# The output projection of the preceding batch, moved in among the transposes of an attention stage

## The reference

```python
x = x + L0_ffn(L0_cond(x, cond_256))     # attention, then a product-key expert layer
x = x + L1_ffn(L1_cond(x, cond_256))     # two small mixtures of 8 experts
```

```python
qkv = (x @ Wqkv.T + bqkv)                       # 16 heads of 8 channels
attn = softmax(q @ k.T / sqrt(8))               # 128 x 128 for each head and batch
coh = sigmoid(tanh(concat(x, cond) @ Wc1.T + bc1) @ Wc2.T + bc2)
mod = attn * coh / (sum(attn * coh) + 1e-8)
mod = 0.79 * mod + 0.21 * fa                    # fa: one row of weights per batch
out = (mod @ v).reshape(B, S, E)
return out @ Wout.T + bout                      # the output projection
```

## Time and profile before

| | us |
|---|---|
| median of three runs | 833.32 |
| the profiled execution | 831.08 |
| its span, first to last instruction | 829.3 |
| TensorE busy | 777.6 |
| weight loads busy | 688.5 |
| VectorE busy | 547.5 |
| ScalarE busy | 579.4 |
| GpSimd busy | 316.6 |

### The profile page before, as it was taken

The page is one execution under the profiler, slowest core; times in us unless marked ns, Lnnn a source line. Parts: engine busy times, 40 slices in busy tenths (PEclk is TensorE's granted clock), DMA queues, the critical chain, the costliest instruction groups (busy, mean ns, idle before and its releaser), DMA issues.

```text
span 829.3 us, 14537 instructions
## 1 busy us (share of the span) xinstructions
PE 777.6 (94%) x5194; PEld 688.5 (83%) x5194; DVE 547.5 (66%) x1450; ACT 579.4 (70%) x990; POOL 316.6 (38%) x231
## 2 busy tenths in 40 slices
PE   4999999897885799999999999999999999999998
PEld 2878878765884688989998898999899999899987
DVE  3566566445806897797697779769778875853522
ACT  2566666523986978896898789789778888753353
POOL 2122221114994936442472753446066362000000
PEclk9899999998897799999999999999999999999999
DMA  9930000000000000000000000000000000000000
GB/s 308 326 89 2 1 2 2 1 1 0 2 1 0 1 2 1 8 1 2 1 8 1 2 8 1 1 2 7 1 1 8 1 2 8 0 2 1 8 1 7
DMA packets 11015, 16.92 MB, mean 20 GB/s; under 512 B 664, under 2 KB 6976, under 8 KB 10688
## 3 DMA queue, kind: packets, MB, share of 16 engines
q1 hardware_dynamic: 10944, 15.99, 6.1%
HBM read 14.94 MB, written 1.05 MB: 19 GB/s over the span
## 4 chain that ended last, share of the span: by engine, by line
PE 83%; POOL 8%; issue 4%; DVE 3%; ACT 2%; DMA 1%; DVEq 0%; SPq 0%; ACTq 0%; POOLq 0%
PE banks L441 76%; POOL region L390 7%; PE banks L480 4%; PE banks L639 2%; ACT x1T_all L885 1%; ACT G_both L876 1%; DMA region<-in_pC 1%; DVE HF L1320 0%; PE banks L494 0%; PE banks L671 0%; DVE W_both L1314 0%; DVE W_both L1145 0%; PE banks L730 0%; DVE acc L1455 0%; PE banks L652 0%
## 5 line engine op out<-in xcount | busy, mean ns | idle before, releaser
L390 POOL TENSOR_TENSOR region<-sim 128x1024 f32<-128x1024 f32 x128 | 260.7, 2064 | 101.5 <-DVE top_keys L1271 63.6
L1003 ACT ACTIVATE HF<-banks,lpack 128x256 f32<-128x256 f32 x256 | 105.6, 480 | 55.4 <-PE banks L441 54.5
L938 ACT ACTIVATE region<-region,neg_thr 128x1024 f32<-128x1024 f32 x128 | 143.7, 1152 | 0.2 <-POOL region L390 0.2
L1314 DVE SCALAR_TENSOR_TENSOR W_both<-region,rz_rel,W_both 128x1024 f32<-128x1024 f32 x98 | 136.8, 1396 | 1.5
L441 PE MATMUL banks<-HF,w_sb 128*128 128x256 f32 x512 | 123.0, 384 | 8.6 <-DVE HF L1320 8.6
L441 PEld LDWEIGHTS banks<-f_sb,HF 128*128 128x128 f32 x1024 | 123.7, 192 | 3.4
L944 ACT ACTIVATE region<-region,dtop 128x1024 f32<-128x1024 f32 x114 | 125.6, 1145 | 0.6
L441 PE MATMUL banks<-f_sb,HF 128*128 128x128 f32 x1024 | 124.5, 275 | 0.0
L441 PE MATMUL banks<-cT,f_sb 128*128 128x256 f32 x512 | 122.7, 382 | 0.1
L441 PEld LDWEIGHTS banks<-HF,w_sb 128*128 128x128 f32 x512 | 94.6, 193 | 20.2 <-DVE HF L1320 9.0
L441 PEld LDWEIGHTS banks<-cT,f_sb 128*128 128x128 f32 x512 | 92.1, 190 | 16.3 <-issue 2.9
(11 more groups left out here) (157 smaller groups left out, 1032.4 us busy)
## 6 DMA issues: line engine op xcount, KB each, us to landing
w_sb<-in_w SPq DMA_DIRECT2D x1, 2048.0 KB, 14.0
f_sb<-in_f SPq DMA_DIRECT2D x1, 2048.0 KB, 14.4
region<-in_wq SPq DMA_DIRECT2D x1, 1024.0 KB, 9.6
region<-in_wqT SPq DMA_DIRECT2D x1, 1024.0 KB, 11.7
w_sb<-in_w SPq DMA_DIRECT2D x1, 1024.0 KB, 9.7
out_x<-acc_f SPq DMA_DIRECT2D x16, 64.0 KB, 1.6
region<-in_pA SPq DMA_DIRECT2D x1, 860.5 KB, 4.8
x1T_all<-in_xT SPq DMA_DIRECT2D x1, 768.0 KB, 8.6
```

The costliest lines, as they stand in the source:

```text
L390: pool.tensor_tensor(S[a][h].rearrange("p (i j) -> p i j", i=NK), sim[a][:, h, :].unsqueeze(2).broadcast_to([P, NK, NK]), sim[a][:, PH + h ...
L938: act.activation(S[a][h], S[a][h], ACT.Prelu, bias=neg_thr[t % 4][:, h:h + 1], alpha=STEEP).then_inc(h_L, 1)
L1003: m = act.activation(HF[e % 2][:, f, :], bank(2 + b, 256 * (f % 2), 256 * (f % 2) + 256), ACT.Gelu_apprx_tanh, bias=L("bf", 4 * e + f, 4 * ...
L1314: v.scalar_tensor_tensor(W[a], S[a][h], rz_rel[a][:, h:h + 1], W[a], ALU.mult, ALU.add).then_inc(h_w, 1)
```

## The change

One call moves on TensorE and one on ScalarE. `out_proj(b - 1)` is now issued inside `transposes(b, 1)`, after its fourth transpose (g = 3), and no longer after the eighth. On ScalarE `out_x1(b - 1)` stands directly after `out_T(b - 1)`, ahead of `probs_T(b, 1)`. No wait and no semaphore is changed; the guard `b > 0` takes the place of `not first`. The projection of the last batch, after the loop, is as before.

```diff
                 for g in range(8):
                     m = pe.transpose(bank(g // FG, P * (g % FG), P * (g % FG) + P), D[q][:, P * g:P * g + P], A("ident"))
+                    if g == 3 and q == 1 and b > 0:
+                        out_proj(b - 1)
                 m.then_inc(s_T, 1)
...
                 transposes(b, 1)
-                if not first:
-                    out_proj(b - 1)
                 if project_more:
...
                 probs_T(b, 0)
                 if not first:
                     out_T(b - 1)
+                    out_x1(b - 1)
                 probs_T(b, 1)
-                if not first:
-                    out_x1(b - 1)
```

## The result

The changed kernel took 823.24 us (median of 4 runs, 821.65 to 825.48), the kernel before 833.30 us (median of 4, 830.81 to 833.34): 10.1 us less, ratio 0.987 with a 95% interval of 0.984 to 0.991. The forecast was 822 (818 to 827) and a gain of 10.0 us. The profiled execution took 821.65 us, with a span of 819.9.

What follows compares the result with a forecast made beforehand. TensorE was taken as the bound, waiting each attention batch for ScalarE's `out_x1`. Per batch 0.68-0.08 = 0.60 us, times 13 = 7.8, plus 1.06 and 1.14, gives 10.0 us less: 822 us, between 821.0 and 823.3, range 818 to 827.

Steps and rivals of the forecast that it cites:

- What the wait costs: TensorE's wait for `out_x1` ahead of the `ones` matmul, attention stage: 0.68 us lost per batch, by the weight loads' pitch.
- The rival of the visible idle: Attention stage: only idle in the matmul rows counts, 0.44 us per batch, not 0.68; 825.6 us; chance 0.08.
- Part 1, the stall: `out_proj`, moved among the transposes, waits on TensorE for `oT`: 0.08 us per batch, bounds 0 and 0.21.
- Part 2, the additional changes between transposes and matmuls: TensorE switches twice more per batch between transposes and full matmuls: costs nothing, at most 0.02 us a change.
- Part 3, `out_x1`: On ScalarE `out_x1` comes first, read by 62.15; the `ones` wait goes, with 0.46 us to spare.
- Part 4, the cover of the later probability copy: ScalarE's probability copy of heads 8 to 15 starts 0.30 us later; cost nothing, without cover 0.3 us a batch.
- Part 5, what is late next: Period shrinks by 0.60 us; VectorE, GpSimd and ScalarE, idle 2.33, 3.84 and 1.92 us, shift along; none becomes the bound.
- Batches 14 and 15: Last two attention batches gain 1.06 and 1.14 us, keeping a wait of some 0.4 us each.
- A later stage changes its length: Rival: stages after attention meet more or less low clock, plus or minus 3.4 us; chance 0.08 for 825 to 828.
- low stretches: Stretches at 1.2 GHz within 170 to 295 us, said not to move along with the work when it comes earlier.
- Slower: Rival: late `oT` stalls TensorE between transposes 3 and 4, deciding from 0.68 us; example 1.03 us late gives 838; chance 0.04.
- The sum: Attention-stage gain over batches 1 to 15: 7.8+1.06+1.14 = 10.0 us.

Runs made afterwards that it cites:

- e1: Kernel before with only the ScalarE half: `out_x1` directly after `out_T`, `out_proj` still after the eighth transpose; 822.6 us, ratio 0.985 to before.
- e3: Changed kernel with `out_proj` after the fifth transpose in place of the fourth; 822.9 us, ratio 0.985 to before.
- e4: Changed kernel with `out_proj` after the first transpose in place of the fourth; 826.2 us, ratio 0.990 to before.
- e6: Changed kernel with `out_proj` after the sixth transpose and the next batch's value copy and tanh moved behind `out_T`'s copy; 820.5 us, ratio 0.984 to before.
- e2: Kernel before with only the TensorE half: `out_proj` after the fourth transpose, ScalarE's order as before; 838.5 us, ratio 1.005 to before.
- e5: Changed kernel plus an extra 128x1024 ScalarE copy ahead of `out_T`'s copy in every batch but the first, making `oT` late; 833.0 us, ratio 0.998 to before.

## Why the prediction was right

- *What the wait costs.* 0.68 us from the pitch of the loads, not the 0.44 shown as idle. e1, which takes the wait away and leaves TensorE's order alone, shortens the period by 0.685. The rival of the visible idle is out.
- *Part 1, the stall.* Forecast 0.08 us (0 to 0.21); measured 0.083, as 8.486 less 8.403 of e3. Four kernels, which differ in the place of `out_proj` or the arrival of `oT`, have stalls of 0, 0.08, 0.41 and 0.75 us, and periods of 8.403, 8.486, 8.813 and 9.157: each tenth of stall is a tenth of period.
- *Part 2, the additional changes between transposes and matmuls.* Nothing, by e3 against e1: 8.403 and 8.401.
- *Part 3, `out_x1`.* Read by 60.93, 1.46 us after the transposes' start, forecast 62.15-60.70 = 1.45. The `ones` load could start 0.11 us behind that, at 61.04, and its turn is at 61.49, so the room is 0.45 us for the 0.46 worked out.
- *Part 4, the cover of the later probability copy.* It starts 0.30 us later and the probability values never wait for it. In e4 it starts 1.76 us after the first transpose (62.35-60.59), ScalarE no longer waits for VectorE ahead of the exponentials, and still the period is the sum of the stalls.
- *Part 5, what is late next.* No other engine became the bound at 8.49, nor at 8.31 in e6. ScalarE's wait for GpSimd fell from 1.92 to 1.31 us with the period.
- *Batches 14 and 15.* 1.04 and 1.13 us for 1.06 and 1.14; they keep a wait of some 0.4 us each, as given: 0.44 and 0.44 by the loads. The idle time ahead of the matmuls is only 0.2 each (0.4 in 2 waits) and again understates it.
- *A later stage changes its length.* Between the two profiled executions it did not. In others it does, by up to some 5 us (e1 660.3 and e2 660.2 us from the first subtraction to the end, before and changed 655.5), so the rival describes what spreads the runs, not what the change does. That the two profiles have the same length behind the stage, to 0.02 us, is luck. The step of the prediction by which the low stretches "don't move along with the work" was wrong: they moved along (above).
- *Slower.* The break-even at a stall of 0.68 us held by e5. The example in the prediction has a slip: `oT` late by 1.03 us adds to the stall of 0.08 that is there already, so it would be 1.11-0.68 = 0.43 us a batch, not 0.35.
- *The sum.* 10.0 us forecast, 9.97 in the stage, 10.1 between the medians. The last agreement is partly luck, since the runs of each kernel spread by 2.5 to 3.8 us. Which half brings the gain was not asked beforehand, and the answer is unequal: ScalarE's order brings 10.3 us of it alone (136.14 to 125.85); TensorE's order alone costs 4.35, and on top of the other it costs 0.3 (125.85 to 126.17), or gives 0.6 where `out_proj` comes one transpose later (e3, 125.23).

## What to carry to other kernels

When one engine's stream stops for another, take the pitch at which its instructions start, and compare the start behind the stop with the turn that it would have had; the idle time in brackets was less than the loss here (0.44 for 0.68 us), because the records overlap. A result that a waiting engine needs goes ahead of a long copy that nobody is waiting for; the order of the copying engine may be the whole change. Moving the producer forward gains nothing as long as that copy stands ahead of its result (e2), and moved past the arrival of its own input it costs, one for one (e4).

## What the runs showed of the hardware

- A load of TensorE that waits for ScalarE's semaphore alone starts 0.05 us after the end of ScalarE's record, in every batch in which it waited (`out_proj` in the changed kernel, e4 and e5). Ahead of the `ones` load the trace has a semaphore instruction of TensorE's sequencer with two of the waits, and there it is 0.11 us, in all 15 batches of before. A waiting load holds the loads behind it (0.33 us in e4, 0.72 in e5).
- An activation that waits for nothing else starts 0.10 to 0.13 us before the recorded end of the one ahead of it on ScalarE, so a copy of 1.07 us takes 0.95 us of ScalarE's time (60.14 to 61.09 in e5).
- At the beginning of the changed kernel's trace the loads of transposes are 0.21 us apart up to 26.7 us, double the 0.11 of later ones, while the table of stretches gives a granted clock of 1.00 for 0 to 27.6 us. In the trace of before the same loads are as far apart, and there the clock from 20 to 25 us is 0.50. So in the changed kernel's trace the spacing shows the lower level, and the clock column doesn't.
